# Graph attention: a running maximum made for 12 groups of edges at once, weights read from PSUM, a ring of 24 groups

## The chip, the cores and the metric

One core of a Trainium2 chip. The metric is the device time of one execution in microseconds (us), the median of several runs. An execution computes two graph layers over 6250 nodes and 206250 edges sorted by their destination.

## The reference

```
# layer 0 (H = 8 heads of 16)
m      = leaky_relu(xl[src] + xr[dst] + edge_attr @ W_e, 0.2)
logits = einsum('eho,ho->eh', m, att)
lmax   = segment_max(logits, dst)
exl    = exp(logits - lmax[dst])
out    = segment_sum(xl[src] * exl, dst) / segment_sum(exl, dst) + b_att
x      = layernorm(x + layer_norm(h + ffn(h)))     # h = layer_norm(x + out)
# layer 1: a convolution over the same edges: rows gathered by src,
# weights from a small network, segment_sum by dst, then a node update
```

Any shift that is the same for all edges of a node gives the same quotient, so the maximum may be taken over a part of the node's edges, if the sums made so far are multiplied by a factor when it changes.

## The kernel before, in words

The program has five stages one behind the other: `set_up` (node tables xl and xr, indices, limits), `attention`, `update_nodes`, `convolution`, `finish_nodes`. In `attention` (L314 on) the edges come in 403 groups of 512 (four tiles of 128). Every engine runs its own program over steps k; at step k it works on group k - lag, with a lag of its own for each kind of work (`steps`, L85: some steps written out, a loop of 12, a tail of 7). The engines meet by semaphores alone, and an engine's instructions go in the order in which they are written.

- SP loads for each group the indices (L384, once the rows of six groups before are gathered), the relative destinations `rel` (L393), the edge attributes (L395), a window of xr (L399) and the limits (L406).
- POOL gathers for each group the rows xl[src] with four indirect DMAs (L423) into a ring of NX = 12 groups; a gather waits until the message of 12 groups before is made.
- PE adds up the pre-activation of group k - 1 in PSUM: attributes by W_e (L444), the window by a one-hot matrix (L448), and the gathered rows transposed (L456). It makes the logits of group k - 3, 8 rows by 512 edges (L438), the sums of group k - 6 by a one-hot matrix (L466), and transposes the 72 rows of `stack` for group k - 4 (L474).
- ACT makes 0.2 x the pre-activation (L500), copies the logits into `stack` (L487), makes the masks (four times L492, then L495), copies peaks and factor (L505, L507), and takes the exponential of the shifted logits (L512).
- DVE makes the one-hot matrix of the window (L531), the leaky activation (L590), and the maximum: edges of a node lie next to each other, so a forward scan with a limit of plus or minus 1e30 (L551) followed by a reverse scan (L562) leaves each node's maximum at each of its edges. The forward scan carries on from the group before; what the maximum changed by at the group's first node goes into a factor (L569, L578), by which the node's sums so far are multiplied (L558). L594 subtracts the maxima, L584 makes the message (rows times weights), and L544 adds the group's sums to the accumulator, in two parts. The message lags 5 steps, the additions 7.

```
nc.vector.tensor_tensor_scan(stack[0:H, s, ::-1], limit[:, b, GE:0:-1], prefix[:, s, ::-1], ...)   # L562
nc.vector.tensor_tensor(m[:, :, 0:O], xl_rows[...], m[:, :, O:OX].broadcast_to(...), ALU.mult)      # L584
```

The branch with one window for a group (`wins == 1`) is the one that these data take. `set_up` makes the limits on DVE (L285, L289), and SP stores them (L199) before the stage ends; L293 and L294 make index tables, L301 the differences of first and last destinations.

## Time and profile before

| | us |
|---|---|
| median of 3 runs | 4748.86 (4747.91 to 4751.28) |
| span of the profiled execution | 4739.3 |
| first gather of the attention's rows starts | 84.8 |
| last one starts | 2388.5 |
| busy in the span: PE, DVE, ACT, POOL | 3573.2, 3943.6, 2149.4, 3526.2 |

The profile gives of the profiled execution the span from the first to the last instruction; its whole time is not given apart, and the runs' median lies 9.6 us above the span. Busy times count instructions that work; waits and register instructions don't count, nor does the issue of DMAs. An indirect DMA on POOL is an exception: its busy time is that in which POOL writes its descriptors, and its data move later.

### The profile page before, as it was taken

Reading aid. Unit: us, or ns where it says so; the run is one execution under the profiler, and the core shown is the slowest. Engines: PE = TensorE matmul, PEld = TensorE weight load, DVE = VectorE, ACT = ScalarE, POOL = GpSimd, SP = SyncE. Lnnn points to the kernel's source line nnn. Section 1 sums busy time; section 2 is a strip of 40 time slices with the busy share of each in tenths; the row PEclk is TensorE's granted clock in tenths of the full one; section 3 lists DMA queues with packets and bytes.
Section 4 is the critical chain, followed back from the end, with each engine's and each line's share of the span. In section 5 each row is a group of like instructions: output and inputs, shape, how many; then the busy total and the mean of one; then the engine's idle time right before and its main releaser. Section 6 shows DMA issues by size and latency. Waiting matters only on the chain. (4 is left out here: it accounts for less than half of the span.)

```text
span 4739.3 us, 94508 instructions
## 1 busy us (share of the span) xinstructions
PE 3573.2 (75%) x16055; PEld 2271.9 (48%) x16055; DVE 3943.6 (83%) x9690; ACT 2149.4 (45%) x6581; POOL 3526.2 (74%) x3353
## 2 busy tenths in 40 slices
PE   4777777777777777777767777877777777777776
PEld 2333433334344333434345555555555555555555
DVE  5998998998999989999988777777777777777776
ACT  2666666666666666666643222222222222222222
POOL 3777777777777777777756677777777777777774
PEclk7999999999999999999989899999999999999999
DMA  6444444444444444444411222222222222222221
GB/s 191 125 121 125 124 121 125 124 122 125 125 121 124 125 121 125 124 125 122 130 35 38 78 55 55 56 56 56 55 54 55 56 55 56 55 55 55 55 56 50
DMA packets 448082, 430.21 MB, mean 91 GB/s; under 512 B 247916, under 2 KB 339824, under 8 KB 447354
## 3 DMA queue, kind: packets, MB, share of 16 engines
q1 hardware_dynamic: 344698, 216.78, 17.5%
q0 software_dynamic: 103168, 211.49, 17.1%
q14 instruction: 196, 1.61, 0.1%
q8 instruction: 20, 0.33, 0.0%
HBM read 411.13 MB, written 16.78 MB: 90 GB/s over the span
## 5 line engine op out<-in xcount | busy, mean ns | idle before, releaser
L423 POOL DMA_INDIRECT attn_xl_rows<-xl,attn_idx x1612 | 1813.6, 1125 | 521.7 <-issue 491.1
L959 POOL DMA_INDIRECT conv_rows<-feat,conv_idx x1612 | 1558.4, 967 | 511.8 <-issue 488.5
L975 PE MATMUL conv_sums_ps<-conv_vals,conv_onehot 128*128 128x256 f32 x3224 | 836.0, 404 | 430.7 <-DVE conv_vals L1068 425.1
L1006 ACT ACTIVATE conv_scaled<-conv_w_ps,conv_edge 128x64 f32<-128x64 f32 x1612 | 374.8, 315 | 1446.9 <-PE conv_w_ps L982 1446.9
L975 PEld LDWEIGHTS conv_sums_ps<-conv_vals,conv_onehot 128*128 128x128 f32 x3224 | 598.4, 195 | 658.8 <-issue 576.7
L1057 DVE TENSOR_TENSOR conv_dots<-conv_rows,conv_edge 128x384 f32<-128x384 f32 x403 | 224.9, 558 | 480.1 <-DMA conv_rows<-feat,conv_idx 479.9
L492 ACT ACTIVATE attn_far<-c_iota,c_minus_pos 128x128 f32<-128x128 f32 x1612 | 515.1, 390 | 10.2
L444 PE MATMUL attn_pre_ps<-attn_attrT,c_W_e 128*128 128x512 f32 x806 | 475.6, 673 | 48.3 <-DMA attn_xr_win<-xr_parts 48.3
L551 DVE TENSOR_TENSOR_SCAN attn_prefix<-attn_limit,attn_prefix,attn_logit_ps 8x512 f32<-8x512 f32 x403 | 508.3, 1261 | 0.0
L474 PE MATMUL attn_stackT_ps<-c_ident,attn_stack 72*128 72x72 f32 x1612 | 191.9, 243 | 417.0 <-DVE attn_stack L578 416.6
L562 DVE TENSOR_TENSOR_SCAN attn_stack<-attn_limit,attn_prefix 8x512 f32<-8x512 f32 x403 | 486.2, 1207 | 0.1
L466 PE MATMUL attn_sums_ps<-attn_msg,attn_onehot 128*128 128x136 f32 x3224 | 447.5, 282 | 0.9 <-DVE attn_msg L584 0.9
L438 PE MATMUL attn_logit_ps<-attn_leaky,c_att_block 128*8 128x512 f32 x806 | 429.9, 616 | 2.9
L982 PE MATMUL conv_w_ps<-c_Wp,conv_hid 128*128 128x256 f32 x1612 | 428.1, 389 | 0.0
L466 PEld LDWEIGHTS attn_sums_ps<-attn_msg,attn_onehot 128*128 128x128 f32 x3224 | 408.6, 193 | 4.2 <-DVE attn_msg L584 2.5
L456 PE MATMUL attn_pre_ps<-c_ident,attn_xl_rows 128*128 128x128 f32 x1612 | 261.1, 285 | 162.6 <-DMA attn_xl_rows<-xl,attn_idx 161.1
L456 PEld LDWEIGHTS attn_pre_ps<-c_ident,attn_xl_rows 128*128 128x128 f32 x1612 | 187.7, 143 | 404.3 <-DMA attn_xl_rows<-xl,attn_idx 339.2
L474 PEld LDWEIGHTS attn_stackT_ps<-c_ident,attn_stack 72*128 72x128 f32 x1612 | 136.7, 144 | 490.9 <-DVE attn_stack L578 490.6
L982 PEld LDWEIGHTS conv_w_ps<-c_Wp,conv_hid 128*128 128x128 f32 x1612 | 317.8, 197 | 48.2 <-ACT conv_hid L1012 1.3
L444 PEld LDWEIGHTS attn_pre_ps<-attn_attrT,c_W_e 128*128 128x128 f32 x806 | 125.0, 195 | 409.1 <-issue 360.4
L505 ACT ACTIVATE attn_peaks<-attn_stackT_ps 128x32 f32<-128x32 f32 x403 | 79.7, 198 | 509.5 <-PE attn_stackT_ps L474 469.9
L584 DVE TENSOR_TENSOR attn_msg<-attn_xl_rows,attn_msg 128x512 f32<-128x512 f32 x403 | 288.8, 717 | 12.6
(137 smaller groups left out, 5972.1 us busy)
## 6 DMA issues: line engine op xcount, KB each, us to landing
attn_attrT<-in_attrT SPq DMA_DIRECT2D x403, 256.0 KB
attn_rel<-rel_group SPq DMA_DIRECT2D x403, 126.0 KB
attn_xl_rows<-xl,attn_idx POOLq DMA_INDIRECT x1612
conv_rows<-feat,conv_idx POOLq DMA_INDIRECT x1612
conv_radial<-in_radialT SPq DMA_DIRECT2D x806, 8.0 KB
attn_xr_win<-xr_parts SPq DMA_DIRECT2D x403, 31.5 KB
attn_limit<-limit SPq DMA_DIRECT2D x403, 16.0 KB
attn_idx<-in_src_tiles SPq DMA_DIRECT2D x403, 2.0 KB
```

The lines of the kernel that those rows point to most:

```text
L423: pool.indirect_dma_start(xl_rows[:, b, t, :], None, q["xl"][:, :], bass.IndirectOffsetOnAxis(ap=idx[i][:, t:t + 1], axis=0)).then_inc(row ...
L438: nc.tensor.matmul(logit_ps[:, g.slot(2), :], sb["att_block"][:, :], leaky[:, g.slot(2), :], start=True, stop=True).then_inc(logit_ready, 1)
L444: nc.tensor.matmul(pre_ps[:, g.slot(2), :], sb["W_e"][:, :], attrT[:, b, :], start=True, stop=False)
L456: last = nc.tensor.matmul(pre_ps[:, g.slot(2), t * P:(t + 1) * P], xl_rows[:, g.slot(NX), t, :], ident[:, :], is_transpose=True, start=Fal ...
L466: last = nc.tensor.matmul(to, onehot[:, g.slot(2), t, :], msg[:, g.slot(2), t, :, :].rearrange("p h o -> p (h o)"), start=wins > 1 or t == ...
L492: nc.scalar.activation(far[:, t, :], sb["iota"][:, :], ACT.Abs, bias=sb["minus_pos"][:, bass.ds(g.index(TG, t), 1)]).then_inc(far_ready, 1)
L551: nc.vector.tensor_tensor_scan(prefix[:, s, :], limit[:, b, 0:GE], logit_ps[:, g.slot(2), :], prefix[:, before, GE - 1:GE], ALU.min, ALU.m ...
L562: nc.vector.tensor_tensor_scan(stack[0:H, s, ::-1], limit[:, b, GE:0:-1], prefix[:, s, ::-1], -BIG, ALU.min, ALU.max).then_inc(peak_ready, 1)
L959: pool.indirect_dma_start(rows[:, k.slot(NX), t, :], None, q["feat"][:, :], bass.IndirectOffsetOnAxis(ap=idx[b][:, t:t + 1], axis=0)).then ...
L975: last = nc.tensor.matmul(to, onehot[:, g.slot(2), t, :], vals[:, g.slot(2), t, :], start=wins > 1 or t == 0, stop=wins > 1 or t == TG - 1)
L982: last = nc.tensor.matmul(w_ps[:, g.slot(2), c:TG:2, :], hid2[:, g.slot(2), c * P:(c + 1) * P], sb["Wp"][:, :, :], start=True, stop=True)
L1006: nc.scalar.activation(scaled[:, g.slot(2), t, :], w_ps[:, g.slot(2), t, 0:2 * MUL], ACT.Copy, scale=edge4[:, bass.ds(g.index(TG, t), 1), ...
```

## The change

The 403 groups are put into blocks of 12 (the first has 7). The logits of a block's groups gather in one PSUM bank: each group's matmul has `att_block` in 8 of 96 columns of a padded matrix, and all 12 add up, so that rows 8j to 8j + 7 hold group j. Once in 12 groups DVE scans forward and in reverse on 96 partitions; PE brings the two ends of each group to 8 partitions, DVE scans over the groups, PE hands back what each group has to carry in, and DVE scans forward and in reverse again with that. DVE subtracts, ACT takes the exponential in place, PE transposes the weights into PSUM (`turn_ps`), where they stay. Per group DVE copies the weights of its 8 heads beside the message and multiplies the rows by the weights in PSUM. The factor comes once per block. Messages lag 19 steps, sums 20, additions 21; the ring of rows has 24 groups, the loop 24 steps. Indices are loaded once per block; the attributes lie in the space of `xT`, which nothing else uses in this stage. ACT no longer copies logits, peaks or factor, and `set_up` makes two selection rows (`csel`, `dsel`) and drops `minus_pos`.

```diff
+B = 12
+SPAN = 2 * B
+FIRST = G % B if G % B else B
+SIZES = [FIRST] + [B] * ((G - FIRST) // B)
+WHERE = [(s, j) for s, n in enumerate(SIZES) for j in range(n)]
+ROWS = H * B
...
+            group_first = base_all[0:H, :].rearrange("p (g t) -> p g t", t=TG)[:, :, 0]
+            group_last = last_all[:, :].rearrange("p (g t) -> p g t", t=TG)[:, :, TG - 1]
+            dve.tensor_tensor(same[:, 0, 0:G], group_first, group_last, ALU.is_equal).then_inc(selects, 1)
+            dve.tensor_tensor(same[:, 1, 1:G], group_first[:, 1:G], group_last[:, 0:G - 1], ALU.is_equal).then_inc(selects, 1)
+            dve.wait_ge(selects, 2)
...
-            dve.tensor_scalar(sb["minus_pos"][:, :], dst_tiles[:, :], -1.0, None, ALU.mult)
-            dve.tensor_copy(sb["first_pos"][:, :], base_all[0:H, :])
+            dve.tensor_copy(sb["first_pos"][:, :], group_first)
+            dve.tensor_tensor(sb["csel"][:, :], same[:, 0, 0:G], same[:, 1, 0:G], ALU.mult).then_inc(selects, 1)
...
-        NX = 12
-        NI = 6
+        U = SPAN
+        NX = U
         ND = 4
-        NF = 4
         HX = H * OX
...
-        idx = [tile(f"idx{b}", [P, TG], I32) for b in range(NI)]
+        idx = tile("idx", [P, 2, B * TG], I32)
...
-        attrT = tile("attrT", [P, ND, GE])
+        attrT = sb["xT"][:, 0:ND * GE].rearrange("p (b e) -> p b e", b=ND)
...
-        limit = tile("limit", [H, ND, GE + 1])
+        limit = tile("limit", [ROWS, 2, GE + 1])
...
+        MSG, SUMS, ADDS = B + 7, B + 8, B + 9
+        TAIL = ADDS
         PEEL = G % U + U
...
-                    if live(0):
-                        b = k.slot(NI)
-                        at_least(sp, rows_gathered[k.back(NI).slot(NX)], k.back(NI).uses(NX, 16 * TG))
-                        sp.dma_start(idx[b][:, :], q["src_tiles"][:, bass.ds(k.index(TG), TG)]).then_inc(idx_loaded[b], 16)
...
+                    s, j, n = place(k)
+                    if j == 0:
+                        at_least(sp, max_steps, s.back(1).index(MS))
+                    if j == n // 2 and s.at:
+                        last = k.back(j + 1)
+                        sp.wait_ge(rows_gathered[last.slot(NX)], last.uses(NX, 16 * TG))
+                        load_idx(s.back(-1), k.back(j - n), B)
+                    sp.dma_start(limit[j * H:(j + 1) * H, s.slot(2), :], q["limit"][bass.ds(k.index(GE), GE + 1)].rearrange("(a n) -> a n", a=1)
+                                 .partition_broadcast(H).rearrange("p a n -> p (a n)")).then_inc(limit_loaded[s.slot(2)], 16)
+                steps(sp, G, PEEL, U, 0, body)
...
+                if j == 0:
+                    pool.wait_ge(idx_loaded[s.slot(2)], s.uses(2, 16))
+                    pool.sem_inc(pool_turn, 1)
                 if not isinstance(k.i, int) or k.at >= NX:
                     pool.wait_ge(msg_ready, k.back(NX).uses())
                     pool.sem_inc(pool_turn, 1)
                 for t in range(TG):
                     pool.indirect_dma_start(xl_rows[:, b, t, :], None, q["xl"][:, :],
-                                            bass.IndirectOffsetOnAxis(ap=idx[i][:, t:t + 1], axis=0)
+                                            bass.IndirectOffsetOnAxis(ap=idx[:, s.slot(2), j * TG + t:j * TG + t + 1], axis=0)
...
                     if live(3):
                         g = k.back(3)
+                        s, j, n = place(g)
                         pe.wait_ge(leaky_ready, g.uses())
-                        at_least(pe, prefix_ready, g.back(2).uses())
-                        nc.tensor.matmul(logit_ps[:, g.slot(2), :], sb["att_block"][:, :], leaky[:, g.slot(2), :], start=True, stop=True).then_inc(logit_ready, 1)
+                        if j == 0:
+                            at_least(pe, max_steps, s.back(1).index(MS))
+                        lo = (B - 1 - j) * H
+                        nc.tensor.matmul(logit_ps[0:n * H, s.slot(2), :], att_pad[:, lo:lo + n * H], leaky[:, g.slot(2), :], start=j == 0, stop=j == n - 1).then_inc(logit_ready, 1)
...
-                    if live(6):
-                        g = k.back(6)
+                    if live(SUMS):
+                        g = k.back(SUMS)
...
+                    if closing(k, 5, live):
+                        s, n, _ = closing(k, 5, live)
+                        pe.wait_ge(max_steps, s.index(MS, M_RIGHT))
+                        to = turn_ps[0:n * H, s.slot(2), CHAIN:CHAIN + 2 * B].rearrange("p (a j) -> p a j", a=2)
+                        nc.tensor.matmul(to[:, 0, 0:n], heads_of[:, 0:n * H], left[:, s.slot(2), B - n:B], start=True, stop=True)
...
+                    if closing(k, 7, live):
+                        s, n, _ = closing(k, 7, live)
+                        pe.wait_ge(max_steps, s.index(MS, M_ROW))
+                        pe.wait_ge(exp_ready, s.uses())
                         for t in range(TG):
-                            last = nc.tensor.transpose(stackT_ps[:, t, 0:SX], stack[:, g.slot(2), t * P:(t + 1) * P], ident[0:SX, 0:SX])
-                        last.then_inc(turned, 1)
+                            nc.tensor.transpose(turn_ps[:, s.slot(2), t * ROWS:t * ROWS + n * H], top[0:n * H, t * P:(t + 1) * P], ident[0:n * H, 0:n * H])
+                        nc.tensor.transpose(turn_ps[:, s.slot(2), DROPS:DROPS + H], drop_row[:, :], ident[0:H, 0:H]).then_inc(max_turns, 1)
...
+                if closing(k, 8, live):
+                    s, _, _ = closing(k, 8, live)
+                    act.wait_ge(max_turns, s.index(MT, T_EXP))
+                    nc.scalar.activation(turn_ps[:, s.slot(2), FACTORS:FACTORS + H], turn_ps[:, s.slot(2), DROPS:DROPS + H], ACT.Exp).then_inc(factor_ready, 1)
+                if closing(k, 7, live):
+                    s, n, _ = closing(k, 7, live)
+                    act.wait_ge(max_steps, s.index(MS, M_SHIFT))
+                    nc.scalar.activation(top[0:n * H, :], top[0:n * H, :], ACT.Exp).then_inc(exp_ready, 1)
...
+                if live(MSG):
+                    g = k.back(MSG)
...
+                    if live(ADDS):
+                        n = k.back(ADDS)
+                        s, j, _ = place(n)
+                        first = n.index(2 * wins)
                         block_of = [dve.value_load(sb["tile_block"][0:1, bass.ds(n.index(TG, w), 1)], min_val=0, max_val=BLOCKS - 2) for w in range(wins)]
...
                         at_least(dve, acc_steps, first)
-                        old = acc[:, bass.ds(block_of[0], 1), :, :].rearrange("p b h o -> p (b h) o")
...
+                        if j == 0:
+                            old = acc[:, bass.ds(block_of[0], 1), :, :].rearrange("p b h o -> p (b h) o")
+                            nc.vector.tensor_tensor(old, old, bc(turn_ps[:, s.slot(2), FACTORS:FACTORS + H], 2, OX), ALU.mult).then_inc(factored, 1)
+                            dve.wait_ge(factored, s.uses())
                         dve.wait_ge(sums_ready, n.uses())
...
-                    if live(4):
...
-                    if live(5):
-                        m_of = k.back(5)
-                        dve.wait_ge(exp_ready, m_of.uses())
-                        m = msg[:, m_of.slot(2), :, :, :].rearrange("p t h o -> p (t h) o")
-                        nc.vector.tensor_tensor(m[:, :, 0:O], xl_rows[:, m_of.slot(NX), :, :].rearrange("p t (h o) -> p (t h) o", o=O),
-                                                m[:, :, O:OX].broadcast_to([P, TG * H, O]), ALU.mult).then_inc(msg_ready, 1)
...
+
+                    if closing(k, 7, live):
+                        s, n, g = closing(k, 7, live)
+                        R, b = n * H, s.slot(2)
+                        dve.wait_ge(max_steps, s.index(MS, M_TOP))
+                        nc.vector.tensor_scalar(drop[:, :], left[:, b, B - n:B - n + 1], top[0:H, 0:1], 0.0, ALU.subtract, ALU.min).then_inc(max_steps, 1)
+                        dve.wait_ge(max_steps, s.index(MS, M_DROP))
+                        nc.vector.tensor_tensor(top[0:R, :], logit_ps[0:R, b, :], top[0:R, :], ALU.subtract).then_inc(max_steps, 1)
+                        nc.vector.tensor_scalar(drop_row[:, :], sb["iota"][0:H, :], sb["first_pos"][:, bass.ds(g.back(n - 1).index(), 1)], drop[:, :],
+                                                ALU.is_equal, ALU.mult).then_inc(max_steps, 1)
+                    if closing(k, 6, live):
+                        s, n, _ = closing(k, 6, live)
+                        R, b = n * H, s.slot(2)
+                        dve.wait_ge(max_turns, s.index(MT, T_CHAIN))
+                        chain = turn_ps[0:R, b, CHAIN:CHAIN + 2 * B].rearrange("p (a j) -> p a j", a=2)[:, :, 0:n]
+                        nc.vector.tensor_tensor(picked[0:R, :, 0:n], chain, bc(group_of[0:R, 0:n], 1, 2), ALU.mult).then_inc(max_steps, 1)
+                        nc.vector.reduce_sum(carry[0:R, :], picked[0:R, :, 0:n], mybir.AxisListType.X).then_inc(max_steps, 1)
+                        dve.wait_ge(max_steps, s.index(MS, M_CARRY))
+                        nc.vector.tensor_tensor_scan(turn_ps[0:R, b, :], limit[0:R, b, 0:GE], logit_ps[0:R, b, :],
+                                                     carry[0:R, 0:1], ALU.min, ALU.max).then_inc(max_steps, 1)
+                        dve.wait_ge(max_steps, s.index(MS, M_CARRIED))
+                        nc.vector.tensor_tensor_scan(top[0:R, ::-1], limit[0:R, b, GE:0:-1], turn_ps[0:R, b, ::-1],
+                                                     carry[0:R, 1:2], ALU.min, ALU.max).then_inc(max_steps, 1)
+                    if closing(k, 5, live):
+                        s, n, g = closing(k, 5, live)
+                        b, first = s.slot(2), g.back(n - 1)
+                        before = left[:, 1 - b, B:B + 1]
+                        dve.wait_ge(max_turns, s.index(MT, T_ENDS))
...
+                    if closing(k, 4, live):
+                        s, n, g = closing(k, 4, live)
+                        R, b = n * H, s.slot(2)
+                        dve.wait_ge(limit_loaded[b], lines_in_slot(s))
+                        dve.wait_ge(logit_ready, g.uses())
+                        at_least(dve, factor_ready, s.back(2).uses())
+                        nc.vector.tensor_tensor_scan(turn_ps[0:R, b, :], limit[0:R, b, 0:GE], logit_ps[0:R, b, :],
+                                                     -BIG, ALU.min, ALU.max).then_inc(max_steps, 1)
+                        dve.wait_ge(max_steps, s.index(MS, M_PREFIX))
+                        at_least(dve, max_turns, s.index(MT))
+                        nc.vector.tensor_tensor_scan(top[0:R, ::-1], limit[0:R, b, GE:0:-1], turn_ps[0:R, b, ::-1],
+                                                     -BIG, ALU.min, ALU.max).then_inc(max_steps, 1)
+                        dve.wait_ge(max_steps, s.index(MS, M_LOCAL))
+                        nc.vector.tensor_tensor(ends[0:R, :, 0:n], bc(group_of[0:R, 0:n], 1, 2), bc(top[0:R, 0:GE:GE - 1], 2, n), ALU.mult).then_inc(max_steps, 1)
+                    if live(MSG):
+                        g = k.back(MSG)
+                        s, j, _ = place(g)
+                        if j == 0:
+                            dve.wait_ge(factor_ready, s.uses())
+                        at_least(dve, sums_ready, g.back(2).uses())
+                        to = msg[:, g.slot(2), :, :, :]
+                        weights = turn_ps[:, s.slot(2), 0:TG * ROWS].rearrange("p (t r) -> p t r", t=TG)[:, :, j * H:(j + 1) * H]
+                        nc.vector.tensor_copy(to[:, :, :, O], weights)
+                        nc.vector.tensor_tensor(to[:, :, :, 0:O], xl_rows[:, g.slot(NX), :, :].rearrange("p t (h o) -> p t h o", o=O),
+                                                bc(weights, 3, O), ALU.mult).then_inc(msg_ready, 1)
...
```

## Rows read from the trace of the kernel before

**Rows 1.** The page's costliest groups: the two gathers (busy, mean ns | idle before).

```profile
L423 POOL DMA_INDIRECT attn_xl_rows<-xl,attn_idx x1612 | 1813.6, 1125 | 521.7 <-issue 491.1
L959 POOL DMA_INDIRECT conv_rows<-feat,conv_idx x1612 | 1558.4, 967 | 511.8 <-issue 488.5
```

**Rows 2.** Busy time in a stretch of the attention stage, by engine.

```profile
core 0: us, PE busy (x) PEld busy (x) DVE busy (x) ACT busy (x) POOL busy (x), PEclk, DMA share, GB/s
1000.00:1500.00 500.00, 376.47 (x1830) 199.38 (x1827) 453.27 (x956) 316.21 (x875) 393.35 (x351) 0.97 0.47 123
```

**Rows 3.** Waits of SP's queue in that stretch (us in total, times, longest).

```profile
SPq L384 <- DMA attn_xl_rows<-xl,attn_idx: 195.9, 87, 3.6
```

**Rows 4.** Groups of DVE instructions in that stretch (busy, mean ns | idle before).

```profile
L551 DVE TENSOR_TENSOR_SCAN attn_prefix<-attn_limit,attn_prefix,attn_logit_ps 8x512 f32<-8x512 f32 x87 | 109.7, 1261 | 0.0
L562 DVE TENSOR_TENSOR_SCAN attn_stack<-attn_limit,attn_prefix 8x512 f32<-8x512 f32 x87 | 104.9, 1206 | 0.0
...
L590 DVE TENSOR_TENSOR attn_leaky<-attn_pre_ps,attn_fifth 128x512 f32<-128x512 f32 x87 | 59.2, 680 | 1.2 <-ACT attn_fifth L500 1.2
L531 DVE TENSOR_SCALAR attn_onehotT<-attn_rel,c_window_row 126x512 bf16<-126x512 bf16 x86 | 30.6, 356 | 36.6 <-issue 19.4 <-DMA attn_rel<-rel_group 13.3 <-PE attn_pre_ps L456 3.4
...
L578 DVE TENSOR_SCALAR attn_stack<-c_iota,c_first_pos,attn_drop 8x128 f32<-8x128 f32 x87 | 29.3, 337 | 2.9
...
L558 DVE TENSOR_TENSOR c_acc_attn<-c_acc_attn,attn_factor 128x136 f32 x87 | 22.8, 262 | 0.0
L569 DVE TENSOR_SCALAR attn_drop<-attn_prefix,attn_stack 8x1 f32<-8x1 f32 x87 | 16.7, 192 | 0.0
L594 DVE TENSOR_TENSOR attn_shift<-attn_stackT_ps,attn_peaks 128x32 f32<-128x32 f32 x87 | 15.4, 177 | 0.9 <-ACT attn_factor L507 0.9
```

**Rows 5.** Gathers' own view (ns min/median/max, first and last start us).

```profile
L423 POOL DMA_INDIRECT attn_xl_rows<-xl,attn_idx x1612: 940/946/1924, 84.8 to 2388.5; - x180
```

**Rows 6.** Time line of POOL (start us, duration us, instruction, idle before).

```profile
1510.57 1.30 POOL L423 DMA_INDIRECT attn_xl_rows<-xl,attn_idx  x1 [0.31 <-issue]
1512.17 0.94 POOL L423 DMA_INDIRECT attn_xl_rows<-xl,attn_idx  x1 [0.30 <-issue]
1513.42 1.85 POOL L423 DMA_INDIRECT attn_xl_rows<-xl,attn_idx  x1 [0.30 <-issue]
1515.58 0.94 POOL L423 DMA_INDIRECT attn_xl_rows<-xl,attn_idx  x1 [0.31 <-issue]
```

**Rows 7.** Time line of DVE beside them.

```profile
1510.36 0.69 DVE L584 TENSOR_TENSOR attn_msg<-attn_xl_rows,attn_msg 128x512 f32<-128x512 f32 x1
...
1511.93 1.26 DVE L551 TENSOR_TENSOR_SCAN attn_prefix<-attn_limit,attn_prefix,attn_logit_ps 8x512 f32<-8x512 f32 x1
...
1513.31 1.20 DVE L562 TENSOR_TENSOR_SCAN attn_stack<-attn_limit,attn_prefix 8x512 f32<-8x512 f32 x1
```

**Rows 8.** Time line of the stage's start, POOL and DVE.

```profile
86.27 0.94 POOL L423 DMA_INDIRECT attn_xl_rows<-xl,attn_idx  x1 [0.30 <-issue]
...
106.15 0.35 DVE L531 TENSOR_SCALAR attn_onehotT<-attn_rel,c_window_row 126x512 bf16<-126x512 bf16 x1 [1.67 <-DMA attn_rel<-rel_group]
106.25 1.06 POOL L423 DMA_INDIRECT attn_xl_rows<-xl,attn_idx  x1 [0.30 <-issue]
```

**Rows 9.** Time line of the stage's end, from the last gather to the last addition.

```profile
2388.54 0.95 POOL L423 DMA_INDIRECT attn_xl_rows<-xl,attn_idx  x1 [0.30 <-issue]
...
2400.46 1.28 ACT L492 ACTIVATE attn_far<-c_iota,c_minus_pos 128x128 f32<-128x128 f32 x4
...
2401.77 0.72 ACT L495 ACTIVATE attn_onehot<-attn_far,c_one 128x512 f32<-128x512 f32 x1
...
2403.68 2.18 PE L466 MATMUL attn_sums_ps<-attn_msg,attn_onehot 128*128 128x136 f32 x8
...
2414.14 0.35 DVE L544 SCALAR_TENSOR_TENSOR c_acc_attn<-attn_sums_ps,c_pass_on,c_acc_attn 128x136 f32 x1
```

**Rows 10.** Time line of the setup, DVE.

```profile
65.97 0.87 DVE L301 TENSOR_TENSOR set_span<-set_tile_last,c_tile_base 1x403 f32<-1x403 int32 x1
```

227 lines of the change are left out of this document (105 added, 122 removed).

## The prediction

> **What bounds the kernel now.** I read the page's groups first and looked for an engine whose only idle time is its own issue. In the attention stage that is POOL, which issues the gathers of xl rows. Its 1612 gathers are busy 1813.6 us and idle 491.1 us before them, all of it "issue", 0.305 us each; the sum, 2304.7 us, is the whole time from the first gather's start (84.8) to the last one's end (2389.49) [rows 1, 5, 9]. So no wait for a semaphore holds POOL in the stage, and the stage lasts as long as the gathers plus what comes before and after. The convolution's gathers show the same pattern with 0.967 instead of 1.125 us each [rows 1].
>
> Next the busy times in 500 us of the middle: DVE 453 us, PE 376, ACT 316, POOL 393, to which 107 of issue come [rows 2]. These are 87 groups of edges, 5.7 us each. DVE is the busiest by the shares and looks like the bound, but it sat idle 36.6 us before L531 [rows 4]. SP waits there 195.9 us, 2.25 per group, for gathered rows [rows 3], so the loads have room as well.
>
> Third, how long one gather takes: minimum 0.940, median 0.946, maximum 1.924 us [rows 5]. Most are short; a part of them is stretched, and that makes the mean of 1.125. The time line tells by what [rows 6, 7]. The gather at 1510.57 takes 1.30 and ends at 1511.87; DVE's L584 (the message: two operands, both in SBUF) started at 1510.36, before it, and ended at 1511.05, 0.82 before the gather's end. The one at 1513.42 takes 1.85 and ends at 1515.27; L562 (the reverse scan, both operands in SBUF) ran from 1513.31 to 1514.51, 0.76 before. The gather at 1512.17 started in the middle of L551 (the forward scan, one operand in PSUM, 1511.93 to 1513.19) and takes 0.94. So a gather that starts while DVE holds two SBUF operands waits for that instruction's end and then needs its last 0.8 us; one PSUM operand doesn't hold it.
>
> The start of the stage, before DVE has messages to make, shows POOL by itself: from 86.27 to 106.25 it issues 16 gathers, 1.249 us apart; the one at 106.25 takes 1.06, as L531 (bf16, in SBUF) started beside it at 106.15 [rows 8].
>
> **The change, part by part.**
>
> Gathers. The DVE instructions with two large SBUF operands leave the per-group loop: the message reads its weights from PSUM, the reverse scans read PSUM and come twice in 12 groups, and the successor of L558 comes once in 12 and reads its factor from PSUM. L531 stays. By itself POOL needs 1612 x 1.249 = 2013 us [rows 8] for what takes 2304.7: a gain of 292. What contention remains lies between 0 and the convolution's, (0.967 - 0.944) x 1612 = 37 us, with 0.944 = 1.249 - 0.305 [rows 1, 8]; the 0.12 lost in the first 17 gathers makes 11 over the stage [rows 8]. L531 now follows straight behind L590, which may put it on a gather's start more often, so I take 20. Net -272.
>
> The rows show a tensor_tensor, L584, holding a gather [rows 6, 7]. The Trainium skill, page "SBUF — State Buffer", section "Who interferes with whom", has two statements that pull apart: an instruction with two SBUF inputs contends with a GpSimd instruction that reads SBUF, and, in the probe it reports, tensor_copy stalled a DMA from that queue while tensor_tensor did not. By the first the sum stands; by the second the gathers would gain nothing, which is the last rival's 4782. The trace agrees with the first.
>
> DVE's own work. Per group it loses L551, L562, L578, L558, L569 and L594: 1.261 + 1.206 + 0.337 + 0.262 + 0.192 + 0.177 = 3.44 us [rows 4]. It gains a copy of 32 weights, as long as L594, 0.18. Per 12 groups it gains four scans (4 x 1.24, if 512 elements set their time and 96 partitions cost no more than 8), a 96x512 subtraction like L590, 0.68 [rows 4], and some eight small ones of about 0.25: 7.6 us, 0.64 per group. From 5.2 per group [rows 2] it comes to about 2.6. All of this lies beside POOL's 4 x 1.249 = 5.0 per group and counts 0. Without that cover, DVE would have set the pace at 5.2 before.
>
> PE loses four transposes per group and gains some nine small matmuls in 12; the logit matmul writes 96 rows but moves the same 512 columns. It was busy 4.3 us per group, ACT 3.6 [rows 2], and ACT loses four of its instructions per group. SP loses 11 of 12 index loads and with them the wait for gathered rows in front of its bulk loads [rows 3]; these now wait only for the pre-activations of four groups before, so they go out no later. The index load for the next 12 groups goes out 6 groups ahead. All this is covered by POOL's 5.0 and counts 0.
>
> The ring. A gather waits for the message of 24 groups before instead of 12. Messages lag 19 steps instead of 5, so POOL may run 5 groups (25 us) ahead instead of 7. A step with two wide scans costs DVE about 2.4 + 2.7 = 5.1 us, twice in 12 groups, against that slack. I count 0; its bound is a rival.
>
> The drain. Now 25.0 us pass between the last gather's end (2389.49) and the last addition's (2414.49) [rows 9], in 7 steps. After the change 21 steps remain. The 14 more have only masks, messages, sums and additions. ACT needs 2.03 us for one group's masks (2400.46 to 2402.49), and PE 2.18 for the sums in the drain [rows 9]: 14 x 2.2 = 31 us. Half of that, 15, if each step overlaps fully at PE's quicker rate; 50 at the present drain's pace, 25.0 / 7 = 3.6 per step.
>
> Setup. DVE gains two comparisons like L301 (0.87) ahead of the line that releases the store of the limits, and some short ones; it loses L293 and three quarters of the cast of L294, whose price I put at that of L301 each [rows 10]. If the stage waits for the stored limits this is +2, between 0 and 4. Node update, convolution and output are the same code: 0.
>
> Sum: -292 + 20 + 31 + 2 = -239. The profiled execution's span is 4739.3; the median of the runs is 4748.86, and the 9.6 us between them I take as unchanged. 4749 - 239 = **4510 us**.
>
> **The rivals.**
>
> One holder stays (0.13). The message goes on stretching gathers, because xl_rows in SBUF with a broadcast operand is enough, or the copy, or L531, takes its place. Price: 1.30 - 0.94 = 0.36 us in every second group (the group at 1510.57 is hit, the one with the gather at 1515.58 is not [rows 6]), 0.36 x 201 = 73 us: 4583. Against it: L551, also with one PSUM operand, holds nothing.
>
> The closing chain uses up the ring (0.10). Two scans, a matmul, three small steps, two matmuls, two small steps, two scans, a subtraction, an exponential, transposes, the factor: some 12 us from engine to engine in strict order, with the per-group work of PE and DVE queued behind its waits. If each of the 34 closings costs POOL 4 us in spite of the slack, 136 us: 4646.
>
> The gathers get no shorter (0.05), and the kernel is **slower**: if what stretches them is DVE's presence at all, not its second SBUF operand, POOL's 2304.7 stay and the drain and the setup come on top, 4749 + 33 = 4782. This decides where the gathers' mean falls by less than 33 / 1612 = 0.02 us. The 0.94 us gathers at the start and in L551 speak against it.
>
> That the change doesn't do what it says, because the data take the branch with four windows: L531 writes 126 partitions in the trace [rows 4], as only the branch with one window does, and the data stay the same, so it gets no chance.
>
> **How the numbers follow.** The forecast has 0.72, with its own bounds: at best -292 + 15, 4472; at worst -292 + 37 + 50 + 4, 4548. One holder 0.13 (4583), the chain 0.10 (4646), slower 0.05 (4782). The range 4470 to 4595 takes in the first two, 0.85 together. A measurement of this kernel can tell 0.2%, 9.5 us, from no change. Faster by more are the first three cases, less 0.01 for a chain that costs just what the gathers give: 0.94; within, 0.01; slower, 0.05.
>
> **What would show it.** Right: the gathers' mean 0.95 to 0.97 instead of 1.125, their idle still about 491 and all "issue", first to last gather about 2033 us; four scans in 12 groups on 96 partitions at about 1.25 each; DVE busy near 55% in the stage; some 56 us from the last gather to the last addition. Wrong: POOL waiting for messages (the ring), gathers of 1.3 beside the message or the successor of L531, gathers with the old mean, or scans on 96 partitions much longer than 1.26.

## The result, and the profile after

| | before | after |
|---|---|---|
| median, us | 4748.39 (4 runs, 4745.41 to 4751.28) | 4487.0 (4 runs, 4482.37 to 4488.66) |
| span of the profiled execution, us | 4739.3 | 4486.9 |
| mean granted clock of PE | 0.963 | 0.958 |

The ratio is 0.945 (95% interval 0.9436 to 0.9463): 261 us faster by the medians, 252.4 by the two spans. The forecast was 4510, its range 4470 to 4595.

The page of the changed kernel, first its engines, then its groups, dearest first (busy us, mean ns | idle before and what ended it):

```profile
PE 3380.6 (75%) x14817; PEld 2267.6 (51%) x14817; DVE 2995.1 (67%) x8163; ACT 1716.3 (38%) x5037; POOL 3250.2 (72%) x3353
...
L1051 POOL DMA_INDIRECT conv_rows<-feat,conv_idx x1612 | 1569.4, 974 | 511.3 <-issue 490.8
L484 POOL DMA_INDIRECT attn_xl_rows<-xl,attn_idx x1612 | 1526.3, 947 | 521.1 <-issue 487.4
```

The attention's gathers now take 947 ns instead of 1125, and are no longer the dearest group [rows 1]. Their line by itself:

```profile
L484 POOL DMA_INDIRECT attn_xl_rows<-xl,attn_idx x1612: 940/944/1166, 83.6 to 2100.0; - x180
  issue: 487.4, 1599
  DMA attn_idx<-in_src_tiles: 30.1, 1
  DVE attn_msg L681: 3.7, 12
```

The longest takes 1.17 us, where before the longest took 1.924 [rows 5]. But for one wait of 30.1 us before the first gather, the idle time is again POOL's own issue; the 12 times put down to the message are 0.31 us each, as long as an issue, so no gather waited for the ring. The same 500 us of the middle as in [rows 2], and DVE's groups in them:

```profile
1000.00:1500.00 500.00, 372.19 (x1788) 221.62 (x1787) 282.38 (x712) 252.97 (x615) 378.40 (x400) 0.98 0.51 142
```

```profile
L687 DVE TENSOR_TENSOR attn_leaky<-attn_pre_ps,attn_fifth 128x512 f32<-128x512 f32 x100 | 69.0, 690 | 174.2 <-ACT attn_fifth L570 168.1 <-issue 6.1
L681 DVE TENSOR_TENSOR attn_msg<-attn_xl_rows,attn_turn_ps 128x512 f32<-128x512 f32 x100 | 67.5, 675 | 0.0
...
L642 DVE TENSOR_TENSOR_SCAN attn_turn_ps<-attn_limit,attn_carry,attn_logit_ps 96x512 f32<-96x512 f32 x8 | 10.3, 1284 | 0.3
L645 DVE TENSOR_TENSOR_SCAN attn_top<-attn_limit,attn_carry,attn_turn_ps 96x512 f32<-96x512 f32 x8 | 10.2, 1276 | 0.3
L668 DVE TENSOR_TENSOR_SCAN attn_top<-attn_limit,attn_turn_ps 96x512 f32<-96x512 f32 x8 | 9.7, 1217 | 1.0
L664 DVE TENSOR_TENSOR_SCAN attn_turn_ps<-attn_limit,attn_logit_ps 96x512 f32<-96x512 f32 x8 | 9.7, 1216 | 0.0
```

They hold 100 groups of edges instead of 87: 5.0 us each. DVE works 2.82 us per group and waits for ACT, which waits for PE, which waits for gathered rows. A scan over 96 partitions costs 1.22 to 1.28 us, the same as over 8 (1.21 and 1.26 [rows 4]), and there are four in 12 groups instead of 24.

Where the time went, from the first and last gathers of each stage in the two traces:

| stretch | before | after | difference |
|---|---|---|---|
| to the first attention gather | 84.8 | 83.6 | -1.2 |
| attention gathers, first start to last end | 2304.7 | 2017.3 | -287.4 |
| last of them to the first of the convolution | 228.6 | 253.1 | +24.5 |
| convolution gathers | 2049.4 | 2060.5 | +11.1 |
| the rest | 71.8 | 72.4 | +0.6 |

If 0.944 us is taken as the length of an undisturbed gather, the 1612 of the attention carried 291.9 us above it before, and 4.6 after. This sum over all gathers is called the **excess** below. In the trace of the kernel before nearly every stretched gather ends 0.75 to 0.86 us after one of four DVE instructions. Sorted by them, the 291.9 us are:

| DVE instruction before the gather's end | gathers | excess, us |
|---|---|---|
| L562, the reverse scan | 183 | 139.2 |
| L584, the message | 215 | 77.8 |
| L558, the multiplication by the factor | 203 | 73.1 |
| L531, the window's one-hot matrix | 22 | 1.7 |

### The profile page after: what moved, and what is told of

The parts are those of the page before. It is cut to its first block and busy times, and to the rows that moved or that the text cites. A ratio compares the mean times of both kernels' runs of the same rounds, so it can differ in the third digit from the quotient of the medians.

```text
span 4486.9 us, 82704 instructions
## 1 busy us (share of the span) xinstructions
PE 3380.6 (75%) x14817; PEld 2267.6 (51%) x14817; DVE 2995.1 (67%) x8163; ACT 1716.3 (38%) x5037; POOL 3250.2 (72%) x3353
## 5 line engine op out<-in xcount | busy, mean ns | idle before, releaser
L484 POOL DMA_INDIRECT attn_xl_rows<-xl,attn_idx x1612 | 1526.3, 947 | 521.1 <-issue 487.4
L687 DVE TENSOR_TENSOR attn_leaky<-attn_pre_ps,attn_fifth 128x512 f32<-128x512 f32 x403 | 278.1, 690 | 735.3 <-ACT attn_fifth L570 721.5
L570 ACT ACTIVATE attn_fifth<-attn_pre_ps 128x512 f32<-128x512 f32 x403 | 240.7, 597 | 1024.7 <-PE attn_pre_ps L526 1014.9
L575 ACT ACTIVATE attn_far<-c_iota,c_dst_pos 128x128 f32<-128x128 f32 x1612 | 510.1, 390 | 0.5
L514 PE MATMUL attn_pre_ps<-c_xT,c_W_e 128*128 128x512 f32 x806 | 422.5, 606 | 46.2 <-DMA attn_xr_win<-xr_parts 46.2
L503 PE MATMUL attn_logit_ps<-attn_leaky,attn_att_pad 128*96 128x512 f32 (+1 forms) x806 | 434.7, 622 | 0.0
L536 PEld LDWEIGHTS attn_sums_ps<-attn_msg,attn_onehot 128*128 128x128 f32 x3224 | 425.8, 200 | 15.6 <-issue 10.8
L578 ACT ACTIVATE attn_onehot<-attn_far,c_one 128x512 f32<-128x512 f32 x403 | 290.8, 722 | 14.6 <-PE attn_sums_ps L536 0.2
L1084 PE MATMUL conv_hid_ps<-conv_radial,c_mlp 16*128 16x256 f32 x806 | 281.5, 428 | 14.1 <-DMA conv_radial<-in_radialT 14.1
L1122 DVE TENSOR_TENSOR conv_onehot<-c_iota,c_dst_pos 128x512 f32<-128x512 f32 x403 | 275.9, 685 | 0.8 <-DVE c_acc_conv L1113 0.8
L681 DVE TENSOR_TENSOR attn_msg<-attn_xl_rows,attn_turn_ps 128x512 f32<-128x512 f32 x403 | 272.1, 675 | 0.0
```

What stands on the lines that cost most here:

```text
L484: pool.indirect_dma_start(xl_rows[:, b, t, :], None, q["xl"][:, :], bass.IndirectOffsetOnAxis(ap=idx[:, s.slot(2), j * TG + t:j * TG + t + ...
L503: nc.tensor.matmul(logit_ps[0:n * H, s.slot(2), :], att_pad[:, lo:lo + n * H], leaky[:, g.slot(2), :], start=j == 0, stop=j == n - 1).then ...
L514: nc.tensor.matmul(pre_ps[:, g.slot(2), :], sb["W_e"][:, :], attrT[:, b, :], start=True, stop=False)
L536: last = nc.tensor.matmul(to, onehot[:, g.slot(2), t, :], msg[:, g.slot(2), t, :, :].rearrange("p h o -> p (h o)"), start=wins > 1 or t == ...
L575: nc.scalar.activation(far[:, t, :], sb["iota"][:, :], ACT.Abs, bias=sb["dst_pos"][:, bass.ds(g.index(TG, t), 1)], scale=-1.0).then_inc(fa ...
L578: nc.scalar.activation(onehot[:, g.slot(2), :, :], far[:, :, :], ACT.Relu, bias=sb["one"][:, :], scale=-1.0).then_inc(onehot_ready, 1)
```

## The experiments

Two theories: the **port** (a gather that starts while DVE works on two SBUF operands waits for that instruction's end; the operands decide), and the **load** (DVE's amount of work, or the maximum made per group, decides). One definition serves all runs: an instruction *covers* a gather's start if it began at least 0.03 us before it and ended at least 0.15 us after; a covered gather is *held* if it takes over 1.0 us.

The first eight runs went to two chips on which the engines stood still again and again (in the variants of the changed kernel DVE for up to 24 us, PE for up to 21; the kernel before took 6020 and 6144 us, PE's granted clock near 0.80). No run shows why. POOL waited some 700 to 970 us for others in the attention there, so the absolute times answer nothing, and only the lengths of gathers are read. These chips are called disturbed below. The last four runs went to a quiet chip, where the kernel before took 4745.91 us (7 runs), and repeat the important ones.

### Work added to the changed kernel: two SBUF operands, or one

```diff
+ nc.vector.tensor_tensor(extra[:, z.slot(2), :], fifth[:, z.slot(2), :], sb["W1"][:, :], ALU.max)   # a_two_sbuf
+ nc.vector.tensor_tensor(extra[:, z.slot(2), :], pre_ps[:, z.slot(2), :], sb["W1"][:, :], ALU.max)  # a_one_psum
```

> The changed kernel with one more DVE instruction per group, a 128x512 maximum of two SBUF tiles (fifth and the constant W1) into a scratch tile that nothing reads. Theory 'port' (a gather that starts while DVE holds two SBUF operands waits for its end): the message of the kernel before, of the same length, cost about 0.36 us in every second group, so +50 to +110 us, and the gathers' mean rises from 0.947 to 0.98 to 1.02 us. Rival 'load' (the gathers became shorter because DVE has less to do): DVE goes up by 0.7 us per group here as in the next run, and both runs change alike. Rival 'nothing left' (POOL covers it all): both within 5 us of the changed kernel, 4487.

> The same extra DVE instruction, of the same size and at the same place, but with its first operand in PSUM (pre_ps in place of fifth). Theory 'port': one SBUF operand holds nothing, so the gathers' mean stays at 0.945 to 0.955 and the time within 8 us of 4487. Rival 'load': it slows the kernel as much as the run with two SBUF operands does.

Measured on the disturbed chip: ratios to the kernel before 0.9622 (0.9544 to 0.9699) and 0.9658 (0.9574 to 0.9742), not to be told apart. Excess of the attention's gathers 15.6 and 4.4 us: the same added work costs gathers only when both operands lie in SBUF. This pair is the cleanest test, as DVE's load is the same in both. With both operands in SBUF the added instruction covered 69 starts and held 54; the other 15 were stretched as well (0.96 to 0.99 us) and ended 0.82 after it. With one operand in PSUM it covered 60 and held none. The gathers' mean, 0.954 us, stayed under the 0.98 to 1.02 expected, as only those 69 fell under it. The ring in both profiles:

```profile
L485 POOL DMA_INDIRECT attn_xl_rows<-xl,attn_idx x1612: 938/944/1458, 82.8 to 2879.0; - x180
...
  DVE attn_msg L682: 772.3, 179
```

```profile
L485 POOL DMA_INDIRECT attn_xl_rows<-xl,attn_idx x1612: 941/947/1167, 83.5 to 2860.5; - x180
...
  DVE attn_msg L682: 766.4, 175
```

The longest gather takes 1458 ns with two operands in SBUF, 1167 with one. The first, again, on the quiet chip:

> The changed kernel plus one DVE maximum a group over two SBUF operands whose result nobody reads (work added, output unchanged). On an undisturbed chip (before at about 4750 us): port theory: the attention's gathers carry 10 to 30 us of excess instead of 4.6 and the time is 4487 + 5 to 30 us, ratio 0.946 to 0.952. Load theory: DVE rises by about 0.3 us of 5.0 a group and is no bound, so nothing changes, ratio 0.945.

Measured: 4525.39 us, ratio 0.9528 (0.9508 to 0.9548), 38 us above the changed kernel. Excess 51.4 us, more than the 10 to 30 expected from the disturbed chip: there POOL often stood waiting, and 69 starts fell under the instruction where now 151 do. The port theory's upper end for the time (30) was passed as well; the load theory's 0 is out by more. DVE and POOL side by side in this run:

```profile
1507.12 0.69 DVE L688 TENSOR_TENSOR attn_extra<-attn_fifth,c_W 128x512 f32<-128x512 f32 x1 [1.46 <-ACT attn_fifth L571]
1507.21 1.42 POOL L485 DMA_INDIRECT attn_xl_rows<-xl,attn_idx  x1 [0.30 <-issue]
...
1513.32 0.68 DVE L689 TENSOR_TENSOR attn_leaky<-attn_pre_ps,attn_fifth 128x512 f32<-128x512 f32 x1
...
1513.93 0.94 POOL L485 DMA_INDIRECT attn_xl_rows<-xl,attn_idx  x1 [0.30 <-issue]
...
1514.81 0.67 DVE L682 TENSOR_TENSOR attn_msg<-attn_xl_rows,attn_turn_ps 128x512 f32<-128x512 f32 x1
1515.17 0.95 POOL L485 DMA_INDIRECT attn_xl_rows<-xl,attn_idx  x1 [0.30 <-issue]
```

The added instruction (both operands in SBUF) ends at 1507.81, and the gather that began under it ends 0.82 later. The message, as long and with one operand in PSUM, covers a gather's start too, and that one takes 0.95. Over the stage the added instruction covered 151 starts and held 140; the message covered 129, of which 13 were held, the leaky activation 171, of which 2 were held. In all 13 the added instruction stood directly behind the message and began 0.11 to 0.12 us after the gather, which ended 0.82 after it; so these are its own as well. Of the 11 that the added instruction covered and didn't hold, 6 were stretched to 0.97 to 0.99 and ended 0.82 after it; 5 began only 0.03 to 0.04 after it and took 0.94.

### The weights back in SBUF

```diff
-nc.vector.tensor_copy(to[:, :, :, O], weights)
+nc.vector.tensor_copy(to[:, :, :, O], weights).then_inc(copied, 1)
+dve.wait_ge(copied, g.uses())
...
-                        bc(weights, 3, O), ALU.mult).then_inc(msg_ready, 1)
+                        bc(to[:, :, :, O], 3, O), ALU.mult).then_inc(msg_ready, 1)
```

> The changed kernel, but the message multiplies the rows by the weights copied to SBUF (two SBUF operands, as before the change) after a wait for the copy. Theory 'port': +50 to +110 us, gathers of 1.2 to 1.6 us that end 0.8 us after the message. Rival 'block' (the gain comes from the maximum made once in 12 groups and the fewer instructions, not from where the weights are read): within 8 us of 4487.

Measured on the disturbed chip: 0.9673 (0.9586 to 0.976); excess 44.4 us.

> The same kernel as a_weights_sbuf, again, as the first call's chip ran every kernel some 27% slower, with stops of up to 17 us on all engines, so that only the gathers' lengths could be read there (0.972 us each against 0.947 for the run with the PSUM operand). On an undisturbed chip, theory 'port': the message's holds cost POOL 40 to 110 us, gathers' mean 0.97 to 1.02, ratio to the kernel before 0.953 to 0.968. Rival 'block': the ratio stays at 0.945.

Measured on the other disturbed chip: 0.9556 (0.9505 to 0.9608); excess 39.1. The time expected was for an undisturbed chip, which came third:

> The changed kernel with only the weights put back into SBUF: copied there, and the message multiplication has two SBUF operands again. Port theory: on an undisturbed chip (before at about 4750 us) the attention's gathers carry 35 to 60 us more than the changed kernel's 4.6 us of excess and the time is 4487 + 35 to 60 us, ratio 0.952 to 0.958. Load theory (DVE busy 56% is too little to hurt): no change, ratio 0.945. If the weights' place were the whole cause of the gain, the kernel would return to 1.0.

Measured: 4531.53 us (4528.91 to 4534.29), ratio 0.9548 (0.9532 to 0.9564): 44.5 us above the changed kernel, in the range. Excess 54.4:

```profile
L485 POOL DMA_INDIRECT attn_xl_rows<-xl,attn_idx x1612: 940/944/1472, 85.3 to 2151.6; - x180
  issue: 489.0, 1604
```

The message covered 204 starts and held 196, each to 0.82 us after its end; in the changed kernel it covered 188 and held none. DVE's work is nearly the same (694 ns for the message instead of 675), so the rival 'block' of the first expectation, no change, is out. The stage's length follows the gathers: 2067.3 us against 2017.3, +50.0.

The run also says how much is not the message's. With its weights in SBUF the kernel still takes 214 us less than the kernel before (4531.53 against 4745.91). The larger part of the gain thus comes with the rest of the change. The trace points to the maximum made for 12 groups at once, which takes L562 and L558, the holders of 212 of the 291.9 us, out of the work per group. No run made the maximum for 12 groups with all operands left in SBUF, so how that part divides between fewer instructions and their new operands wasn't measured.

### The port theory on the kernel before

```diff
-nc.scalar.activation(msg[:, g.slot(2), :, :, O], shift[:, g.slot(2), :, :], ACT.Exp).then_inc(exp_ready, 1)
+nc.scalar.activation(w_ps[:, g.slot(2), :, :], shift[:, g.slot(2), :, :], ACT.Exp).then_inc(exp_ready, 1)
...
+nc.vector.tensor_copy(m[:, :, O], weights)
-                        m[:, :, O:OX].broadcast_to([P, TG * H, O]), ALU.mult).then_inc(msg_ready, 1)
+                        bc(weights, 2, O), ALU.mult).then_inc(msg_ready, 1)
```

> The kernel before with this one part of the change: ACT writes the exponentials to a free PSUM bank, DVE copies them beside the message and multiplies from PSUM. DVE has 0.2 us per group more to do. Theory 'port': the message's hits vanish (215 gathers x 0.36 = 77 us), of which the reverse scan and the factor may take back a part, as the gathers then start at other moments: 20 to 80 us faster than 4748. Rival 'load': 0 to 80 us slower, as DVE's step of 5.2 us grows by 0.2.

Measured on a disturbed chip: 0.9832 (0.9758 to 0.9907), 96 us less than the kernel before there, from which little follows; excess 173.9, against 291.9 in the undisturbed kernel before. The message covered 175 starts and held none, the reverse scan, still with both operands in SBUF, 170 and held 162. With the scans moved as well, the maximum still being made once per group on 8 partitions:

```diff
-nc.vector.tensor_tensor_scan(prefix[:, s, :], limit[:, b, 0:GE], logit_ps[:, g.slot(2), :], prefix[:, before, GE - 1:GE], ALU.min, ALU.max)
+nc.vector.tensor_tensor_scan(logit_ps[:, s, :], limit[:, b, 0:GE], logit_ps[:, s, :], last_col[:, before, :], ALU.min, ALU.max)
...
+nc.vector.tensor_copy(last_col[:, s, :], logit_ps[:, s, GE - 1:GE])
-nc.vector.tensor_tensor_scan(stack[0:H, s, ::-1], limit[:, b, GE:0:-1], prefix[:, s, ::-1], -BIG, ALU.min, ALU.max)
+nc.vector.tensor_tensor_scan(stack[0:H, s, ::-1], limit[:, b, GE:0:-1], logit_ps[:, s, ::-1], -BIG, ALU.min, ALU.max)
```

> The kernel before with two operands moved to PSUM: the message's weights (as in b_weights_psum) and the forward scan, which now writes over the logits in PSUM, so that the reverse scan has one SBUF operand; a small copy keeps its last column. Maximum still per group on 8 partitions, ring of 12, message lag 5. Of the two-SBUF instructions only L558's (factor) and L531 stay. Theory 'port': the gathers' mean falls from 1.125 to 0.96 to 1.02 us; POOL alone would then need 2040 to 2140 us for the stage, but DVE's step grows from 5.2 to about 5.5 us per group with the two copies, 403 x 5.5 = 2217 us, so DVE becomes the bound and POOL waits for messages: 50 to 130 us faster than before (ratio 0.973 to 0.990). Rival 'load': 40 to 150 us slower than before.

Measured on a disturbed chip: 0.9891 (0.9837 to 0.9944), excess 31.0. On the quiet one:

> The kernel before, its maximum still once per group on 8 partitions, with the weights and the scanned logits in PSUM, so that neither the message nor the scans read two SBUF operands, and DVE does as much work as before. Port theory: the attention's gathers keep about 31 us of excess against 291.9 before, and POOL is no longer what bounds the stage: DVE's chain of 5.2 to 5.6 us a group does, so that the kernel gains only 50 to 130 us (ratio 0.973 to 0.990). Load theory: the gathers keep their 1.125 us mean and the ratio is 1.0. Then the reduced DVE work of the changed kernel is what turns short gathers into time.

Measured: 4789.76 us (4787.07 to 4796.46), ratio 1.0089 (1.0072 to 1.0106), 0.9% **slower** than the kernel before. The port theory's gain of 50 to 130 us didn't come. Of the time the load theory was nearer: 1.0 was written for it here, 40 to 150 us slower for the run before this one, and 44 were measured. But its mechanism isn't what happened. The gathers did get shorter (989 ns instead of 1125, excess 73.3; the message covered 268 starts and held none, the reverse scan 99 and none), at 91% of DVE busy, but POOL now waits. The gathers' line, SP's queue in 1000 to 1500 (waits: us, times, longest), and that window:

```profile
L425 POOL DMA_INDIRECT attn_xl_rows<-xl,attn_idx x1612: 938/944/2007, 85.7 to 2414.3; - x180
  issue: 501.4, 1484
  DMA attn_idx<-in_src_tiles: 265.7, 128
```

```profile
SPq L408 <- DVE attn_stack L582: 203.1, 85, 7.9
```

```profile
1000.00:1500.00 500.00, 364.92 (x1793) 202.86 (x1791) 455.53 (x1109) 302.03 (x853) 335.15 (x340) 0.94 0.46 120
```

DVE is busy 91%, as in the kernel before, with 85 groups in the window: 5.88 us each, 5.36 of it work. SP can't load limits before DVE has finished an earlier group, and the next indices stand behind that in SP's queue; so DVE's pace reaches POOL. The stage's gathers take 2329.5 us, 24.8 more than before: 218.6 less excess, and 243 of new waits (174 gaps of 296.6 us, less 0.305 each). After the last gather 13 groups instead of 7 remain, and 55.9 us instead of 25.0. What excess is left comes from L561, the multiplication by the factor, with both operands in SBUF, straight behind the forward scan: 188 of the 256 gathers begun under that scan were held.

So DVE is a second bound close behind the first, and with the maximum per group shorter gathers alone didn't make this kernel faster. How close it is in the kernel before itself isn't shown: the variant has two copies per group that the kernel before lacks (0.213 us for the weights, 0.134 for the last column), 140 us over 403 groups. An estimate that takes them off gives 5.78 - 0.35 = 5.43 us per group for DVE's pace over the stage, against POOL's old 5.72; a repair without copies might have gained something like that difference, some 115 us over 403 groups, less the 30.9 us by which the drain grew. The changed kernel shortens the gathers and takes DVE off the path, at 2.82 us per group.

### Longer lags

```diff
-        MSG, SUMS, ADDS = B + 7, B + 8, B + 9
+        MSG, SUMS, ADDS = B + 11, B + 12, B + 13
```

> The changed kernel with message, sums and additions 4 steps later (lags 23, 24, 25 instead of 19, 20, 21), so that POOL may run ahead 1 group instead of 5, and the drain has 4 steps more. Theory of the drain (ACT's masks set its pace, 2.06 us per step): +8 us. Ring: in the changed kernel POOL waited for a message only twice in 500 us; with one group of slack every closing step of DVE (up to 6 us) and every turn of the loop should make it wait: +20 to +250 us. If the ring has nothing to do with the time, +8 us alone.

Measured on a disturbed chip: 0.9492 (0.9433 to 0.9551). POOL waits 764.7 us for the message:

```profile
L484 POOL DMA_INDIRECT attn_xl_rows<-xl,attn_idx x1612: 942/947/1167, 83.3 to 2862.1; - x180
  DVE attn_msg L681: 764.7, 154
```

The variant with one PSUM operand, with the lags as they were, waited 766.4 us on the other disturbed chip. So four steps more added nothing to be seen beside the waits that these chips bring, and this run says nothing about four lags on a quiet chip, where POOL doesn't wait at all. Inconclusive.

### The same remedy in the convolution

The convolution's code is the same in both kernels, yet its gathers took 11.1 us longer in the changed one. The longest gathers there are held by L1122, the mask of the destinations, whose two operands (row numbers and positions) both lie in SBUF. Two short instructions, L1154 and L1156, hold gathers too, and cost less (5.5 and 7.3 us of the excess of 47.7, against 33.6). POOL and DVE in the changed kernel:

```profile
3003.72 0.69 DVE L1122 TENSOR_TENSOR conv_onehot<-c_iota,c_dst_pos 128x512 f32<-128x512 f32 x1
3003.79 1.43 POOL L1051 DMA_INDIRECT conv_rows<-feat,conv_idx  x1 [0.30 <-issue]
```

The mask starts 0.07 before the gather, ends at 3004.41, and the gather 0.81 later. 69 starts were covered and 69 held, against 49 of 49 before; 20 more at 0.49 us are 9.8 of the 11.1 us. The edit takes the row numbers from PSUM:

```diff
+dve.tensor_copy(iota_ps[:, :], sb["iota"][:, :]).then_inc(zeroed, 1)
...
-nc.vector.tensor_tensor(onehot[:, g.slot(2), :, :], bc(sb["iota"][:, :], 1, TG),
+nc.vector.tensor_tensor(onehot[:, g.slot(2), :, :], bc(iota_ps[:, :], 1, TG),
```

> The changed kernel, with one line of the convolution changed too: its one-hot comparison (128x512) reads the row of column numbers from a PSUM copy instead of SBUF. In the changed kernel 69 of the convolution's gathers last 1.4 us instead of 0.94, all where a comparison runs over their start, 69 x 0.46 = 32 us. Theory 'port': 10 to 35 us faster than the changed kernel (4452 to 4477), these 1.4 us gathers gone. Rival: unchanged within 5 us, as other instructions with two SBUF operands take its place.

Measured on a disturbed chip: 0.9524 (0.9475 to 0.9573); excess of the convolution's gathers 287.4 us, of which gathers of over 2 us made most (183 of them), so that only the class around 1.4 could be read: 15 instead of 47 to 69. On the quiet chip:

> The changed kernel with the convolution's comparison reading its row numbers from PSUM instead of SBUF, so that only one of its two inputs lies in SBUF. On the first chip where this ran the convolution's 1.4 us gathers fell from 47 to 69 down to 15, but other stops hid what it brings. If the chip's other engines run undisturbed (the kernel before at about 4750 us): by the port theory the convolution's gathers lose most of their excess of 47.7 us and the kernel takes 10 to 40 us less than the changed one (ratio to before 0.937 to 0.943); by the theory that DVE's load or the gather's own variation makes them long, the excess stays at 35 us or more and the ratio stays at 0.945. If the chip is disturbed as the first two were, the ratio says little and the gathers of 1.4 us remain the reading.

Measured: **4457.17 us** (4454.21 to 4458.65), ratio 0.9392 (0.9376 to 0.9407). The convolution's excess fell from 47.7 to 17.5 us, its gathers from 2060.5 to 2030.2 us, and the kernel is 29.8 us faster than the changed one. The same moment in this run:

```profile
3049.57 0.68 DVE L1124 TENSOR_TENSOR conv_onehot<-conv_iota_ps,c_dst_pos 128x512 f32<-128x512 f32 x1
3049.63 0.94 POOL L1052 DMA_INDIRECT conv_rows<-feat,conv_idx  x1 [0.30 <-issue]
```

The instruction is as long and starts as far ahead of the gather, and the gather takes 0.94. All 28 gathers whose start it covered stayed under 1.0 us. This version beats both kernels. By how much the edit itself does it is less sharp than 30 us: four other profiles with the old mask have convolution gathers of 2046.6 to 2052.5 us (listed below), and against the shortest of them the gain is 16 us.

## Why the prediction was right, point by point

**What bounds the kernel.** Right: POOL's gathers, by their own length, and the stage shrank with them. But "without that cover, DVE would have set the pace at 5.2 before" was said in passing, and it is half of the story: with the maximum per group and neither the message nor the scans as holders, a group took 5.88 us in the window and 5.78 over the stage, more than POOL's old 5.72 (2304.7 / 403), though 0.35 of it are the variant's own copies. The 5.2 were DVE's busy time (453.27 / 87) and left out its waits. The prediction credits the gathers alone; that they could turn into time needed DVE's work per group to fall as well, which it counted as 0.

**Gathers: forecast -272, measured -287.4.** The term of the contention was mis-sized: 20 us taken, 4.6 measured, below even the 11 read from the stage's start. L531 (now L602) is the one holder left; it covered 76 starts and held 37, and since it is short (0.36 us) no gather of the stage takes more than 1.17 us. The reading that operands decide stood in every run: two in SBUF held 215 of 221, 183 of 185, 196 of 204, 140 of 151, 69 of 69; one in PSUM 0 of 188, 0 of 268, 0 of 99, 0 of 60, 0 of 28, and the leaky activation 1 of 110. The exceptions with one operand in PSUM are the forward scan (158 of 365 before, 188 of 256 in the variant with both in PSUM) and the 13 of 129 above; in them the holder was the instruction directly behind. The rule of the Trainium skill, page "SBUF — State Buffer", section "Who interferes with whom", that two SBUF inputs contend with a GpSimd instruction reading SBUF, agrees with all of these; the other statement there, of a tensor_tensor that doesn't stall, doesn't hold for these gathers. Here the prediction misread a row. It took one gather under L551 as proof that L551 "holds nothing", though 158 of the 365 gathers that began under L551 were stretched, by 73.1 us in all. It knew L558 as an instruction with two operands in SBUF, but not as the holder of these: L558 runs straight behind L551, and gathers that begin under L551 are held by it, though its record starts later. From the kernel before:

```profile
1527.63 1.26 DVE L551 TENSOR_TENSOR_SCAN attn_prefix<-attn_limit,attn_prefix,attn_logit_ps 8x512 f32<-8x512 f32 x1
...
1528.52 1.39 POOL L423 DMA_INDIRECT attn_xl_rows<-xl,attn_idx  x1 [0.30 <-issue]
1528.82 0.26 DVE L558 TENSOR_TENSOR c_acc_attn<-c_acc_attn,attn_factor 128x136 f32 x1
```

The gather ends at 1529.91, 0.83 after L558, which began 0.3 us later than it. 203 gathers end that way. Of the 168 that began under L551 and at most 0.40 us before L558, 158 were held; of the 197 that began earlier, none. And the wide scan L642 of the changed kernel, which has the same kinds of operands as L551 and no L558 behind it, covered 27 starts and held none. Since the change takes L558 out of the group too, the forecast came out of it unharmed.

**DVE's own work: forecast 2.6 per group, measured 2.82**, and hidden as said. Scans over 96 partitions at 1.22 to 1.28: right (1.24).

**The ring and the closing chain: forecast 0, measured 0.** POOL never waited. In the drain the whole chain lies bare, from the first wide scan to the factor:

```profile
2110.47 1.22 DVE L664 TENSOR_TENSOR_SCAN attn_turn_ps<-attn_limit,attn_logit_ps 96x512 f32<-96x512 f32 x1
...
2118.60 1.27 DVE L645 TENSOR_TENSOR_SCAN attn_top<-attn_limit,attn_carry,attn_turn_ps 96x512 f32<-96x512 f32 x1
...
2124.41 0.16 ACT L561 ACTIVATE attn_turn_ps<-attn_turn_ps 128x8 f32<-128x8 f32 x1
```

14.1 us, where some 12 were estimated, against a slack of 25. On the disturbed chips, where DVE stands for up to 24 us at a time, POOL did wait for messages.

**Drain: forecast +31, measured +26.3** (51.3 us from the last gather's end, 2100.97, to the last addition's, 2152.24, instead of 25.0), and 1.8 less in the update after it. 20 additions remained, not 21, so 13 more than before, at 2.0 each: ACT's masks, 2.06 us from one to the next, set the pace.

```profile
2126.60 1.28 ACT L575 ACTIVATE attn_far<-c_iota,c_dst_pos 128x128 f32<-128x128 f32 x4
...
2128.66 1.28 ACT L575 ACTIVATE attn_far<-c_iota,c_dst_pos 128x128 f32<-128x128 f32 x4
...
2151.89 0.35 DVE L621 SCALAR_TENSOR_TENSOR c_acc_attn<-attn_sums_ps,c_pass_on,c_acc_attn 128x136 f32 x1
```

**Setup: +2 forecast, -1.2 measured. Convolution: 0 forecast, +11.1 measured**, the largest miss of sign. That DVE's mask held gathers there was in the rows (0.967 instead of 0.944); that their number can change with the code unchanged was not thought of (69 starts covered by the mask instead of 49; that the two engines merely stand differently against each other is the reading, no run shifted them on purpose). The convolution's gathers took 2049.4, 2060.5, 2049.4, 2052.5 and 2046.6 us in five quiet profiles (before, after, weights back, work added, both in PSUM) with the same code, and 47, 69, 45, 50, 39 of them were between 1.4 and 1.5 us long.

**The sum.** The terms came to -239; the traces give -252.4 (15.4 from the gathers, 6.5 from the drain and update, 3.2 from the setup, less 11.1 and 0.6). The other 9.6 us of the 23 between 4510 and 4487 are the distance from span to median, taken as unchanged. That was luck of the draw, not a cost of the kernel: in every run on record the time lies only 1.7 to 1.8 us above the core's span (4488.66 and 4486.9 after the change). The profiled execution of the kernel before, with 4739.3, was thus a quick one of some 4741 us, and the profiled one after the change the slowest of its four. Its runs on the quiet chip do range from 4737.26 to 4751.34 us.

**The rivals.** One holder stays: not here, but the run with the weights back in SBUF is that case, at +44.5 us where 73 were priced; the number of gathers was right (203, where 201 were taken), but each lost 0.26 us on average, not the 0.36 of the one that was read. The chain stalls the ring: no; on disturbed chips POOL waited for messages, and no run tells what part of that the chain had. Gathers get no shorter: no.

## What to carry to other kernels

When an engine that issues gathers is the bound, look at the spread of one gather's length, not its mean, and find what DVE was doing when the long ones began; moving one of two large operands of that DVE instruction to PSUM is cheap and took 16 to 30 us off the convolution here. Look at the instruction behind the one that ran when the gather began, too. Before crediting such a repair, work out the pace of the next engine with its waits and the queues behind it, not its busy time alone, and count what the repair itself adds: here the repaired kernel ran into DVE at 5.8 us a group against 5.7, 0.35 of it the repair's own copies, and was slower. Code that is not changed can still gain or lose 10 us, so a difference of that size in one profile is no evidence for an edit elsewhere.

## What the runs showed of the hardware that was not expected

- An instruction with both operands in SBUF holds a gather before its own recorded start, if it stands directly behind another one: L558 held gathers that began up to 0.4 us earlier. In the variant with both operands in PSUM, L561 held 13 that began up to 0.92 us earlier; why so much longer there stays open.
- A DVE instruction that began 0.02 us before a gather didn't hold it: in the run with work added the one at 1512.65 (0.74 us, both operands in SBUF) runs beside a gather at 1512.67 that takes 0.95. Nor did the five there that began 0.03 to 0.04 before theirs. DVE had been idle in front of all six. The convolution's masks, which began 0.07 to 0.19 before, did, 69 times of 69.
- A held gather ends 0.82 us after the message, the mask or the added instruction, and 0.76 after the reverse scan, whenever it began. An undisturbed one takes 0.944, so it looks as if 0.12 to 0.18 us of it pass before it needs what DVE holds; no run took the gather itself apart.
- L531, a comparison in bf16 whose other operand is one number for each partition, holds gathers too (end 0.82 after it), though only one of its operands is large. So "two operands in SBUF" is not the whole condition; no run varied this instruction.
